# Gathers as a stage of their own, new orders for four engines and 728 instead of 1012 spare products, in a 2048-token hybrid block on one core

## The reference, cut to what matters

```python
x = x + L0_attn_a(norm(x))   # gated delta rule with clipping, 16 heads of 8: a scan over the tokens
x = x + L0_ffn(norm(x))      # 2 of 8 experts
x = x + L0_attn_b(norm(x))   # 15 best earlier tokens of each, an MLP on pairs, a palette lookup
x = x + L0_ffn(norm(x))
x = x + L1_attn_a(norm(x))   # linear attention
x = x + L1_ffn(norm(x))      # 2 of 8 experts, shared part
x = x + L1_attn_b(norm(x))   # decaying state
x = x + L1_ffn(norm(x))
```

## Time and profile before

| | us |
|---|---|
| median of 3 runs (lowest, highest) | 1498.96 (1495.59, 1512.79) |
| the profiled execution, span from first to last instruction | 1705.2 |
| busy: PE, DVE, POOL, ACT | 1432.7, 1046.2, 877.8, 836.0 |
| mean granted clock of PE | 0.867 |

### The profile page before, as it was taken

The page is one execution under the profiler, slowest core; times in us unless marked ns, Lnnn a source line. Parts: engine busy times, 40 slices in busy tenths (PEclk is TensorE's granted clock), DMA queues, the critical chain, the costliest instruction groups (busy, mean ns, idle before and its releaser), DMA issues.

```text
span 1705.2 us, 54458 instructions
## 1 busy us (share of the span) xinstructions
PE 1432.7 (84%) x22044; PEld 939.2 (55%) x22044; DVE 1046.2 (61%) x4618; ACT 836.0 (49%) x2249; POOL 877.8 (51%) x1399
## 2 busy tenths in 40 slices
PE   2687878988979897998988889798997979888987
PEld 1243445555656464655656565575755556656664
DVE  2877656775656575576656757567774765464442
ACT  1232333464554454555545555456472545545655
POOL 2447456565636455465455547456554546545331
PEclk8679889987878898898779989788997979798999
DMA  5000010000000000000000000100000010100000
GB/s 151 2 1 26 8 28 17 17 15 18 9 23 5 22 9 15 18 8 20 11 24 8 15 19 6 28 3 23 10 6 25 6 27 10 27 14 20 3 5 6
DMA packets 24294, 30.12 MB, mean 18 GB/s; under 512 B 9089, under 2 KB 18978, under 8 KB 24034
## 3 DMA queue, kind: packets, MB, share of 16 engines
q0 software_dynamic: 8304, 16.73, 3.8%
q1 hardware_dynamic: 15730, 9.82, 2.0%
HBM read 25.21 MB, written 2.29 MB: 16 GB/s over the span
## 4 chain that ended last, share of the span: by engine, by line
PE 64%; DVE 12%; issue 9%; ACT 7%; POOL 3%; another core or an unknown queue 3%; SPq 1%; DMA 0%; DVEq 0%; ACTq 0%; POOLq 0%
PE ps L521 11%; PE ps L757 4%; PE ps L745 3%; PE ps L663 3%; PE ps L715 3%; PE ps L561 3%; PE ps L737 2%; DVE ps L961 2%; PE ps L575 2%; PE ps L585 2%; PE ps L861 2%; PE ps L602 2%; PE ps L853 2%; PE ps L688 2%
## 5 line engine op out<-in xcount | busy, mean ns | idle before, releaser
L521 PE MATMUL ps<-sb 128*128 128x512 bf16 x1012 | 318.7, 423 | 5.4 <-issue 1.2
L961 DVE TENSOR_TENSOR_SCAN ps<-ps,sb 128x47 f32<-128x47 f32 (+3 forms) x1024 | 271.0, 265 | 44.0 <-DVE ps L953 1.0
L1781 POOL DMA_INDIRECT sb<-table,sb x240 | 234.2, 976 | 121.3 <-issue 61.1
L953 DVE TENSOR_TENSOR ps<-sb,ps 128x24 f32<-128x24 f32 (+3 forms) x1024 | 192.3, 188 | 14.8
L1649 POOL TENSOR_TENSOR sb<-sb 128x1 f32<-128x1 f32 x128 | 72.7, 568 | 222.0 <-DVE sb L896 221.4
L521 PEld LDWEIGHTS ps<-sb 128*128 128x128 bf16 x1012 | 95.7, 106 | 95.2 <-issue 38.8
L969 DVE TENSOR_TENSOR sb<-ps,sb 128x32 f32<-128x32 f32 x254 | 46.0, 181 | 119.7 <-PE ps L575 87.4
L745 PE MATMUL ps<-sb 15*32 15x16 f32 x4096 | 69.7, 190 | 48.8 <-issue 48.7
L976 DVE TENSOR_TENSOR ps<-sb,ps 128x12 f32<-128x12 f32 x254 | 40.9, 161 | 107.4 <-PE ps L585 88.6
L585 PEld LDWEIGHTS ps<-sb 32*32 32x32 f32 x2032 | 43.6, 109 | 113.3 <-issue 83.4
L1297 ACT ACTIVATE sb<-sb 128x128 f32<-128x128 f32 x128 | 62.3, 489 | 71.4 <-POOL sb L1651 71.1
(11 more groups left out here) (309 smaller groups left out, 3765.0 us busy)
## 6 DMA issues: line engine op xcount, KB each, us to landing
sb<-table,sb POOLq DMA_INDIRECT x240
sb<-in_cs SPq DMA_DIRECT2D x16, 128.0 KB
table<-sb SPq DMA_DIRECT2D x17, 64.0 KB, 1.5
sb<-in_x SPq DMA_DIRECT2D x4, 256.0 KB, 9.5
sb<-dscr SPq DMA_DIRECT2D x64, 2.0 KB
out<-sb SPq DMA_DIRECT2D x16, 64.0 KB, 1.5
sb<-in_mdn POOLq DMA_DIRECT2D x1, 512.0 KB, 9.3
sb<-in_wex SPq DMA_DIRECT2D x1, 512.0 KB, 6.5
```

The source lines that it names most:

```text
L521: e.matmul(b[:, 0:512], identb[:, :], mup[:, 0:512], start=True, stop=True)
L953: e.tensor_tensor(at(psP, p + ROW - 3 - 2 * m, [ROW, 3], [2, m], [1, 2]), AC[:, row(n, k), :, HIST - 2 * m:HIST].rearrange("p r (a b) -> p ...
L961: e.tensor_tensor_scan(at(psD, 16 + k + COMB * skip, [COMB, 3 * ROW - skip]), at(psP, p + skip, [1, 3 * ROW - skip]), Q[:, i % 32, skip:3 ...
L1781: e.indirect_dma_start(GA[:, k, :], None, table[0:128 * i + 128, :] if i else table0, bass.IndirectOffsetOnAxis(u[:, k:k + 1], 0)).then_in ...
```

## The change

1. `STAGE` has a new stage `h`, "near". On POOL, the 15 gathers leave `pal_` (which keeps six pieces a tile) and become `near`, with the same instructions and waits, under a letter of their own. The other engines have no `h`.
2. `ORDER` of PE, DVE, ACT, POOL and SP is written anew, with as many letters of each stage as before (POOL: 336 `p` become 96 `p` and 240 `h`).
3. `FILL` is written anew: 1012 spares before 374 pieces become 728 before 221.

```diff
-STAGE = {"f": "front", ..., "p": "pal", "m": "mix", ...
+STAGE = {"f": "front", ..., "p": "pal", "h": "near", "m": "mix", ...
 ORDER = {
     "POOL":
-        "ffffggfggggfffggggfgggfffggggggoofooooooofggafggfpgpppppggooppppoooooooggppafppppppgppppfggfppppfopogggooofo"
+        "ffffggfgggfgffgggfgggfffggggggoofoogoogooofggaffgppppgppoggohgoooohhooohahfhhhhghhhghhpgfhgpfpfppoopggohofoo"
...
     "PE":
-        "fsffggsffgsgsssfssgssgfssfssssgsssssgsssssssfssssgsosooossssfssgfossoosssaasasssgasaassasassasgssppsssspsppp"
+        "fffssggffssggsfsssssgfsgsssfsgsssssssssgsfssssssgsossosfossogssossfoosssaasgssasssaassasaassasgspspsssspspfs"
...
 FILL = (
-    "0000000020000002004001000000000000000000000030000200000004070010000000070000002000100060000003104000306000000000"
+    "9290080120203030050200000020000030201010000010100000300400000000200520054200000008710000000000004010002402001090"
...
         def pal_(c):
...
             e.tensor_tensor(nr[:, 4:6], nr[:, 2:4], mhalf[:, 0:2], ALU.pow).then_inc(*p_.G("n2"))
+
+        def near(c):
+            i = c % NT
+            u = p_.u[c % 2]
             for k in range(15):
                 yield
                 w.wait_ge(*m_.P.at(f"t{k // 4}", c - 1))
...
-        stages = {..., "pal": pal_, "mix": mix, ...}
+        stages = {..., "pal": pal_, "near": near, "mix": mix, ...}
```

More of the change, by code:

```diff
@@ L101 @@
 LN_V, LN_G, LN_A, LN_P = ["bs", "ba"], ["lr", "nb"], ["xn", "xt"], ["T"]
-STAGE = {"f": "front", "g": "gram", "s": "scan", "o": "out", "a": "ffn2", "p": "pal", "m": "mix", "b": "ffn4", "l":
+STAGE = {"f": "front", "g": "gram", "s": "scan", "o": "out", "a": "ffn2", "p": "pal", "h": "near", "m": "mix", "b": "ffn4", "l":
          "lin", "c": "ffn6", "d": "dec", "e": "ffn8"}
@@ L115 @@
[L115 to L124, removed]
@@ new lines @@
+        "osgssospossoospsgssssosossasasassfssapssaaaasasfsgspsmmpsgsmmssmmosmpsmmfsoopsmpsmsmsoosmsmmspgsomosfssmmmma"
+        "sssfsaasssmaasagssasmsamsamsgmpmsspsmmsospmsmmsmooossfosmsmmssmspsgmsmoopmsmmmmmasaasgssmmgmmfaapmmssaamsmfa"
+        "pssabbspsbssmpmmmmbsmbbbsmmspbbmsmsmsmlolgsooososllslmmsllfssgsmmmslpolsslmmsmopsmmcmscsccmscaccagscmcspmasm"
+        "sfmsdsdmsaddsmadpsmagfmassasddadgsdbsmssbbpsompmgmsfomobmsmbbpoomsbbbmmsmmslmoslssgmssomlllslsmllpsmgplplmmm"
+        "asmmaccascmcgmscscmmsscpcscsmmfssemsemseesmemeadesaedeadssdaaadpgsfmmdmsdmsmdbdmsmmobbspmmmspmosobosomfbbsbm"
@@ new lines @@
+        "eaesasamaaddosgsddsbmbsbsoooobsmspbbmspbmsmsmbbmsmmmopsolspmplssmsmsllallllmsmaalmslmmmsppcccccsccscceeeeees"
+        "mmsdmasmmaeedsmmaemsdddaaasmmmmsddbddsbbmmompmpboobboobbbmmmmpmmlmmlpmmpllsllloloppmlamalammmmcccccccccaeead"
+        "eaedeemdmdmmmdeaaseadmmmdedbdbbmmmmpmbpbbmmmbbbpmmmmppbpblblmmmmpmmllllllbbbmmbblblmmmlmlccccccllccllllceeel"
+        "edeedlmmdmmdmmemmedemmmmmmcmdcddbdcbmbcmmmmcmmcmmbcbbmcbbbmcmlmldmmdemmeeddlldelllleemmmddemmddemmmlelmmmmcc"
+        "cbccbbccccbbbebeeebbededleldeddlllllleldldddcccccccccedeededededeeddeddeeeeeeeee",
@@ new lines @@
+    "DVE":
+        "fffffssssssssssssssssssfssssssfsssssssssssssssfsssssssssssfssssssssssssssssssssssssssssssssssssssssfsssssfss"
+        "sssssssssssssssssssssssssssssssssssssssssssssssssssssssssssssssssssssssssssssssssssssssssfssssssfsssssssssss"
+        "sssssssssssssssssssssssssssssssfssssssssfsossasssssssssssssssssssssssssssssssssasasaassssssasssssssssassasss"
+        "ssssssssssssssssssassspssssssssssssssssssssssssssssssssssssssssssssssssssspspssssssssssssssssssppspspsssssss"
+        "ssssssssssssssfsssssssssssssssfsssssssssssssssssosssssassssssssssssssssssaasssssssssssssssssasaassssssssssss"
+        "saasssssssssssssssaspsssssssssssfsssssssssssfssssssssssssssssssssssssssssssssssssssssssspsspssssssfsfmssssss"
+        "ssssssssssssssssssssssssosssssssssssssssaspmssssssssmsssssssssssssspsasssssssmpssssfaasassssssassssspsasssss"
+        "assssssssssssssssssssssasssssfspssssssssssssssssssssssssssssssssssssmsssssssssssssssssssssssssssssssssssssss"
+        "ssfsssssssssssfsossssassssspppsspspsssssamsssssssssaaspssssasaasssssssasssssssssmsmsssssabssssspsmssssfsbsss"
+        "sssssbssbbssssssssbssbsbssssfsssssssssssblssssssssssssmssssssssssssssssssssssssssssssssssslsssssssfsfsssslsl"
+        "slslslssssssssssssssssslsssossscssspasssssssssssscssspsspspsscsssmsspsssssssscspsdasasassssssssssasssssssass"
+        "sssssdssssdssdassamfsmsdmsssssssssssssssssasbpsssssssssdsssssssssfsssssssssbsbsbssbsfbssssbssssbsblssfssssss"
+        "sssssssmssssssssssssssssssssssssoasssssssssssslslssllsslssslssslscpsspscsssasssasscsspssssmssssapsspssssssps"
+        "sasssssssssscssessssssssdsssssssssssssssesaesmsmsssassssmsssssasseddasssssssssssdssdbpssfsssssssssssdfssssss"
+        "sbbssssssbssmssbbsssssssssssssbssbssssbsssslsssssssssssssfsssssssfosappssssssssspssssslsslssssslsllmssaslsss"
+        "lscsasassssapsassssssspsssssssasscsssssassmmsssssssssccsesdssssssmssasessspsssssesfbsssssssspsssssssesdsssss"
+        "ssfsssbdssdbbdbbsssmsssbdsbssssssssssblsssssssssssssssssssssssssssssssssssssssfssssssssssssossssfssslasslsls"
+        "llllcsssssssssssssssasspsspcssasssassssmcsssspassssspssssscssssessasdsssssssspapmesaesmsssssssssssdsssssmdab"
+        "sdfssdssssssssesssssssfdsssspssbsssssbbsbbmsssssssbssfssssssssssfbsssssssssssssbsssssslsssssssssssssssssssss"
+        "sssssssoassssspsssspspsssspssslssassssslslslamllssssaaslcssssssssssssssssapsssmcsssssssssmsssfssamscassssssc"
+        "epsssssssssdssassssssbsssessspsssessssssssssfsmsssssssssssdsdssdsdbsssssebssssbssssbssdbsssssfsssssbsbfsssss"
+        "sssbsslsssssssssssssssssssssssssssssossssssmsaslpsspssslplpsllssalassassslpcassssssssasssscsmsssmssssssssssp"
+        "acsmasfsssscessssssdsssassspsssesssssssssbssssssssssssessssssssssssssssssesssssdbssdbsddsbbssssbsssssssssssf"
+        "dsmssssssssssbsbbsslssssssssssssssssssssssssssssssssssssssssosssasssssssssssssssllsssssllsmlsslssssssasalscs"
+        "papasacfssspsspmsssssssmcspmcpessafsssdessssssssessssssssassssssssssssaspsssbsssssssesddbssssssdsssssdsbsbbb"
+        "ssdsssssssssmsssssssbbblsssssssssssssssssssssssfssssssssssssssssfsssossssssssssssssasssssssslsssssslslaslsss"
+        "ssllsasssmlcspssappsassfcspassscsspsssmmassassssssssssmsssssscdspsessasfsssssessssssssessspssbssssssssssssss"
+        "ssssessdssssdsssdssssssssbdbbbbssmdsssbsssbsssssssssssblssssfssssssssssssssssssssssssssssssfsssoasssssssssls"
+        "sssssslsslsllslsssslsscsssssssspsscmpsfpcfsspsssssssssssssssacesssspssdsssssssessssassssasssssmsssessmsssass"
+        "sassssmsssdssdesadssdasssssssssassbsdsspsssssspsssssmsssssssssbsssbbsbbssssssssbssbsssssssbsssfslsssssssssss"
+        "ssfsssosssassssssssssssssssssssssssssssssssssmssllllslssslssssssslscssssssssssssssssscfsmsssssssssssssssssss"
+        "csssssssssssasmsassssssscemsssdssspsappaeeppassmsdddssssssasseasspsdsasssssbsssspssssssdsssssssssssssbssbsbs"
+        "bbssssssssssbssbsssssssssssssssssbslsssssssssssosasssmsssssssssssssssssssslssssslslslsllassssslscmsssssssacs"
+        "spmscsssssmaspsscssepdaeasssssesspssssssspssssasssssasessssssdddabdpsssssssssssspmdssssssssssssbsbbbbbbblmlo"
+        "alllllplcpaacamapmcapcedppameadddedabdbebpbbbmbbbblbbbmbbppbblllllllblcpmpmccplcelldlllpmeeldddecdmbdcbcbbbb"
+        "mbbblcdemmemdddedlllldlllecmbccbbbbbcebbdebleddddllelllllcdcccedeeddddedeeee",
@@ new lines @@
+    "ACT":
+        "ffffffffffffgffsgffffgfffffgsffsfgffgsffgfgffffgsooffofosooofgfoffsaaaaagsaapppgppsppffpofffopsfopgoopoogosp"
+        "aafaaaasafffspfgpmpmfmmgopppfopffpffpooooofsmmmgfomasamfpmffsamfamaapapfggppomspoooffoosfffmmommpppogspppaaf"
+        "gafaaammgmmafmfmffbbmpspbmbbppbspfbmpllollogooololmomflffffmpmgspoplppcfccccapsppccacccccccacgmmaafmpafdsmdd"
+        "dddaffgmmsfmmbgbfbpbbopbfffgffboosopoomoflllmolgmlmlfslpmpppplgpaacccccaacacaccgcmccmccscmeempeefedeeeeeeeem"
+        "eadmeddddpmmfgsfbfbfpbpmobbbppooobosfmoffffomplmlmppllpopgafpllalaasaflsagmmcfcmcacmcccccccmcmcccpfmfmfeeeee"
+        "eedepdeeeeeesbedbdppdbfdpmobbbgpbooolgloloslffmfoffoslflmmlampplpppgcpcaaccaaccfccccagcccmcmcmpmseeepeadeeme"
+        "ededseeeedemdpfdmmeffbfbfbgmpbbbppfoffbffooosoofommgmmpsplolppllppaflaglfaaalapmlgmmccfcmffamcmsccccccccccmc"
+        "mgefeeemeeesepbdepeeeeddeddbdpoebbfbfffpbfooobfoogopsmlmmmlllpopplfpplppmalagaaammpmslacfccgccscffcmfacmcccc"
+        "cccmmeeeeeeeepsddpeeeeeebeddddbbbsbbmgopfpgbooomomololmmplpplsoppplaallfafalapfffapsmmccmfcgcmgcccccccccammc"
+        "cmeeeeemedeseepedeeedeedbdbdppmbbbbpofbgoofomsoooffflmmlmppoppfllppallsalagaapffaffflmgmfmccpcmcgcccccccccca"
+        "mmcmmeseeeeeeeedepeedeeeddbdbdfbpmpbbpsboboooofooflfflgmllmmmossfplpllpppplfffffcpcgacccccccccccamgcmmacsfme"
+        "aeeaeadeeeefgedemeemeeeadsdmdfmdgmobbbpbbbooopbopfoffompfplmomlsspmlplffgfffpplplalmglmmmacpccsccccacccccaam"
+        "mcccfppammeegdegedseeeeeddmedeeedeaemopgbsbbmbbboooopbmopopmppoplpplllspammllalmmaalaacpccmcccmpcccccccccmee"
```

(8 more changed lines are left out.)

134 lines of the change are left out of this document (40 added, 94 removed).

## The result

The changed kernel takes 1610.85 us (median of 4 runs, 1596.18 to 1618.75), the kernel before 1500.22 us beside it: ratio 1.0715, interval 1.0634 to 1.0795. That is slower by 7%; 1465 us and 1427 to 1530 us were predicted.

What follows compares the result with a forecast made beforehand. PE's own instruction list was taken as the limit. Fewer spares gain 53 us, the clock loses 14, gathers and orders count 0: 1705 us become 1666, times 0.879 gives 1465 us, range 1427 to 1530 us.

Steps and rivals of the forecast that it cites:

- The scale: Whole kernel: plain runs are shorter than the profiled span, so 1666 us of span become 1465 us.
- the factor 0.879: Whole kernel: multiplier from profiled span to plain run time, assumed to hold for each term; 1666 us become 1465 us.
- The spares and the clock: On PE: fewer spare products gain 53 us, a clock of 0.85 instead of 0.867 loses 14 us.
- Rival 1: PE's real products: fewer spares lower the clock, a loss below 0.83; at 0.80 1534 us; chance 0.18.
- The orders: All reordered engine lists: pieces move by one place in the median; taken as 0, with 36 us either way.
- Rival 2: Reordered engine lists: new orders wait more, 36 us eat the gain; no change, 1496 us; chance 0.11.
- The gathers: On POOL: fewer gathers right behind a gather save POOL 9 us; taken as 0 at the end, bounds 0 and 9.
- The signs of being wrong: Mean clock under 0.83; PE's middle waits for DVE, ACT or gathers over 90 us; first tile over 10 us longer.
- the first tile: First 100 us: 45 more spares lose 0 to 10 us, taken as 5; over 10 us longer would show error.

Runs made afterwards that it cites:

- The second profile: The kernel before, unchanged, run and profiled again on a chip of the usual kind: 1505.7 us, ratio 0.999, profile span 1499.9 us.

## Why the prediction was wrong

- **The scale (the step that failed first).** "Recording costs this kernel time", and the factor 0.879. The reference profile and the medians came from different kinds of chip. With the span 205 us over the median, the profile was a description of other behaviour, not a stretched picture of the same one. The second profile confirms it: a clock of 0.934 instead of 0.867, and 12.1 and 9.4 us of issue waits at L715 and L745 instead of 28.3 and 48.7.
- **The spares and the clock, 53 - 14 = 39 us gained.** Wrong on both kinds, so the scale isn't what turned the sign: 284 fewer cost 28 us on the usual and 1.4% on the slow one. That they lie on the path was right: 11.0% of the usual chain too. What I priced wrong is what they buy. I gave the clock 14 us, at 0.85; in the old orders it fell from 0.934 to 0.895, and by 1034.9 x (0.934 / 0.895 - 1) that is 45 us. The real products took 71 us longer, all that the spares gave back, and PE idled for 35 us more, which had no term in the sum. Rival 1 named this mechanism, but its threshold (c = 0.83, from a clock of 0.867) didn't hold: on the slow kind the loss was there at 0.841. The forecast also took 64% of the clock's cost and rival 1 all of it. The Trainium skill's page "TensorE: Matmul & The Clock Gate", section "Part 1: The HAM clock gate", which I weighed against the change and priced too low, is borne out by the row of kernels with 1012, 728 and no spares in the old orders: 0.934, 0.895 and 0.800. In the new orders the clocks are 0.894, 0.896 and 0.763, so the number of spares alone doesn't set it.
- **The orders, 0 with 36 us either way.** Rival 2's mechanism with a price of 36 us; measured 65 us with the new spares, 192 us with the old ones and 154 us with none, and a gain of some 75 us on the slow kind. "Pieces hardly moved" (1 place in the median) was no argument: with the new orders alone the waits of the scan's products rose from 8.7 to 42.9 us in the middle.
- **The gathers, 0 to 9 us gained.** Alone, on the usual kind, their places cost 102 us. I wrote that short work behind a gather comes up to a gather earlier or later "in some places", and that a later last gather would cost "a few us a tile", and left both at nothing. In the kernel with the gathers alone moved the waits for both grew: the scale came 85 us later in sum, and POOL's wait for mix's coordinates went from 21.3 to 71.6 us. How much of the changed kernel's time is theirs stays open. (Gathers right behind a gather were 172 before, not 173.) "POOL is 3% of the chain" was true of before and said nothing of a POOL list that is laid out differently.
- **What was forecast rightly.** L521 x728 with 220.5 us (near 230); the chain's share of it 5%, under the 7 to 8%. A span of 1666 us against 1663.8 us on a slow chip is chance: there the spares and the clock, 39 us gained in the sum, cost 1.4%, and the orders, at 0 in it, gave some 75 us.
- **The signs of being wrong.** One came: of PE's 124 us of idle time in the middle of after, 12 us are issue waits and 107 us waits for other engines, over the 90 us named. The clock stayed over 0.83, and the first tile isn't longer: DVE is further in the first 100 us, with 270 instructions against 250.
- One sentence of the kernel's description is wrong: `fill` sets the count anew at every piece, so a digit at a piece without a bank would be lost and not be carried on. No such piece has one; all 1012 and 728 were issued.

## What to carry to other kernels

Before a profile is used as the base of a sum, its span has to agree with the plain runs; where it is 14% off, it shows another state of the machine, and a second one is worth more than any factor. In a kernel whose engines' lists were laid out together, moving one engine's long instructions, however idle that engine is on average, isn't priced by its busy share: what counts is who stands behind them, and what the engine itself then comes to wait for. Two halves of such a change are to be crossed both ways, since each was worth something else beside the other. And filler products on the path are to be priced against the clock that they hold up: take them all out once, and read the clock.

## What the runs showed of the hardware

The same program ran at 1506 us on two chips and at 1708 to 1712 us on three, and two programs changed places: 1506 and 1599 us on one kind, 1708 and 1656 us on the other. TensorE's mean granted clock fell with the fillers in the old orders, 0.934, 0.895, 0.800 for 1012, 728 and 0 of them, while the time moved by 34 us in all. In the traces of the two kernels with moved gathers on chip 1, and in all traces from slow chips but the first, PE's list of products lacks spares: 843 of 1012, or 609 and 607 of 728, although every weight load is there. The changed kernel has all 728 in its trace from chip 7 and 609 in that from chip 2. A missing record isn't a missing product, and PE's busy time in those traces is too low.
